# Twelve blocks on one core: the table that orders all steps, written anew

## What is computed

```python
x = x + _L0_xattn_ref(_layernorm(x, axis=-1), ctx_768, ...)
x = x + _L0_attn_ref(_layernorm(x, axis=-1), ...)
x = x + _L0_ffn_ref(_layernorm(x, axis=-1), ...)
...
x = x + _L3_ffn_ref(_layernorm(x, axis=-1), ...)
return x
```

## Time and profile before

| | |
|---|---|
| median of 3 runs | 2554.51 us (2552.6 to 2557.82) |
| span of the profiled execution, first to last instruction | 2557.4 us |
| the profiled execution against the runs | its span is 2.9 us above their median, inside their range |
| instructions | 62,072 |
| constant products in the table | 588 |

### The profile page before, as it was taken

One profiled execution on the slowest core, in us unless ns is written; L12 is line 12 of the kernel. 1 busy time (PEld: TensorE's weight loads), 2 busy tenths in 40 slices (PEclk: granted clock), 3 DMA queues, 4 the chain that ended last, 5 costly groups with the idle time before them and its releaser, 6 DMA issues.

```text
span 2557.4 us, 62072 instructions
## 1 busy us (share of the span) xinstructions
PE 2254.9 (88%) x26420; PEld 1506.9 (59%) x26556; DVE 1746.6 (68%) x4832; ACT 1368.6 (54%) x2287; POOL 774.0 (30%) x676
## 2 busy tenths in 40 slices
...
GB/s 115 19 41 34 80 45 75 42 24 9 9 11 14 8 8 6 1 47 10 17 16 10 19 25 25 25 16 17 10 11 16 58 8 71 40 55 54 55 104 62
DMA packets 50452, 84.14 MB, mean 33 GB/s; under 512 B 9536, under 2 KB 24768, under 8 KB 49792
## 3 DMA queue, kind: packets, MB, share of 16 engines
...
## 4 chain that ended last, share of the span: by engine, by line
PE 57%; DVE 25%; ACT 8%; issue 4%; POOL 3%; DMA 1%; SPq 1%; another core or an unknown queue 0%; DVEq 0%; POOLq 0%; ACTq 0%
PE psum L946 6%; PE psum L908 5%; PE psum L904 5%; PE psum L1606 3%; PE psum L463 2%; DVE c_L3x_most L1726 2%; PE psum L1699 2%; DVE c_L2x_mx L2081 2%; PE psum L1984 2%; DVE c_L2x_p L2087 1%; PE psum L471 1%; PE psum L1395 1%; PE psum L1976 1%; PE psum L773 1%; PE psum L778 1%
## 5 line engine op out<-in xcount | busy, mean ns | idle before, releaser
L893 POOL TENSOR_TENSOR c_L3f_h<-c_L3f_h,c_L3f_spread 128x512 f32<-128x512 f32 x96 | 121.3, 1283 | 188.8 <-DMA c_L3f_spread<-scratch 103.1
L471 PE MATMUL psum<-halves_held 128*128 128x512 bf16 x454 | 131.0, 403 | 14.0 <-issue 9.8
L936 DVE TENSOR_TENSOR c_L3f_h<-c_L3f_h,psum 128x512 f32<-128x512 f32 (+1 forms) x112 | 75.9, 682 | 76.5 <-PE psum L908 52.0
L922 ACT ACTIVATE c_L3f_h<-psum 128x512 f32<-128x512 f32 (+1 forms) x112 | 65.5, 594 | 110.2 <-PE psum L904 99.1
L946 PEld LDWEIGHTS psum<-weights,c_L3f_h 128*128 128x128 f32 (+1 forms) x896 | 108.1, 193 | 19.3 <-issue 15.3
L946 PE MATMUL psum<-weights,c_L3f_h 128*128 128x128 f32 (+1 forms) x896 | 112.9, 279 | 0.0
L904 PE MATMUL psum<-c_L3f_xT,weights 128*128 128x512 f32 x208 | 107.4, 601 | 0.0
L908 PE MATMUL psum<-c_L3f_xT,weights 128*128 128x512 f32 x208 | 107.4, 603 | 0.0
L471 PEld LDWEIGHTS psum<-halves_held 128*128 128x128 bf16 x588 | 54.3, 102 | 74.8 <-issue 35.1
L893 POOL TENSOR_TENSOR c_L0f_h<-c_L0f_h,c_L0f_spread 128x512 f32<-128x512 f32 x64 | 82.5, 1313 | 50.4 <-DVE c_L0f_h L936 39.2
L1606 PE MATMUL psum<-c_L3x_qx,c_L3x_kT 32*128 32x256 f32 x512 | 77.1, 427 | 21.1 <-DVE c_L3x_most L1726 17.4
...
## 6 DMA issues: line engine op xcount, KB each, us to landing
...
```

The costliest lines, as they stand in the source:

```text
L471: nc.tensor.matmul(j.psum[:, bank, :], j.half["ident"], j.half["take"], start=True, stop=True)
L893: nc.gpsimd.tensor_tensor(h, h, j.m["spread"][:, f, :], ALU.mult).then_inc(*j.up("mixed"))
L922: nc.scalar.activation(j.m["h"][P - rows:P, f, :], j.psum[0:rows, 1 + 2 * f % 3, 0:j.tok], ACT.Silu).then_inc(*j.up("silu"))
```

## The change

Only the string `ORDER` is replaced; no function, tile, size or wait is edited, and `PLAN` stays. Two of its 76 lines, one of each:

```diff
 ORDER = (
-    "vqQDDddDVdldkdddp8paglPLaDKQqDpDDLPaApgApGp7PvvdDavAkGKvvpPPP1paVVa3pgdAdaVpgdVlVPp1pA2PGvQvA4PDadvAkPGPlPvdvkV1pVa3pDDA"
...
+    "dddldVkLqdddDDDDqKQDDvDQLldDppaagkPpaPAgApGppvv3PaAGvvVvpPaPPgpaV3pAdagKVVdVPpA1ppvdPAlvaDdl9PAG2PGvkPvvPDDVpQLVadAa3paa"
...
```

138 lines of the change are left out of this document (69 added, 69 removed).

## The result

The changed kernel takes 2564.64 us (median of 20 runs, 2555.8 to 2577.18), the kernel before 2556.8 us on the same chip (20 runs, 2549.33 to 2563.17). The ratio is 1.0032 with a 95% interval of 1.0019 to 1.0044: **slower by 0.32%, some 8 us**, where 18 us of gain were predicted. Each ratio in this text is an estimate of its own from the single fast executions and can differ from the quotient of the two medians by up to 0.14%; one execution of 3741 us of the kernel before (beside experiments 3 and 4) and one of 4532 us (experiment 7) are left out of the ratios as slow.

What follows compares the result with a forecast made beforehand. TensorE's queue was taken as the bound (busy 2254.9 of 2557.4 us); -2 - 3 - 3 - 6 - 4 = -18 us gave 2539.4, less 2.9 for the median: 2536.5 us, forecast 2525 to 2549, whole range 2508 to 2570.

Steps and rivals of the forecast that it cites:

- place A: Kernel start: removing eight constant products ahead of the first transposes moves all that follows by 2.4 us; taken as -2 us.
- the step that began at 796 us: Sign that the forecast is right: this step is reached some 10 us sooner, with a clock above 0.96 from 332 us.
- Idle time, 302.5 us: Whole span: TensorE idle for 302.5 of 2557.4 us, one of two places where an order of steps can win.
- Products elsewhere, -3: Constant products beyond the start, 0.215 us each: half of those added and removed counts, 4.5 us lost, 7.7 gained.
- The clock, -3 at 17%: Second stretch, 332 to 796 us: half clock cost 6.3 us at 17%; half of it comes back with 42 added products.
- Waits of L1a, -6: TensorE's waits in L1a for `topT` (3.4 us) and the maximum (9.0 us): half of the 12.4 us goes.
- Place B: In L1a, L1246 and sixteen L1254 now stand between L1659 and the first L1606, surely removing its 0.69 us wait for `topT`.
- Transfers and moved issues, nothing: SyncE's queue: transfers moved past each other cost nothing, as each is needed by a job a hundred steps or more later.
- The rest, -4 with ends of +25 and -40: Remaining 290 us of TensorE idleness: as many round trips lose cover as gain it, more lost in L2f; little gain, -4 us.
- The rival by the clock in L2f: Fourth stretch, 1138 to 2058 us: 57 fewer constant products bring more half clock, ending slower at 2571 us; chance 0.15.

Runs made afterwards that it cites:

- experiments 3 and 4: Kernel before with, between 1500 and 2120 us, only the new order (1.0044) or counts (1.0042); or new steps 6860 to 7719 (0.9970), also with new start (0.9977).
- experiment 7: Kernel before without its eight starting constant products (1.0029) or with seven (0.9990); changed kernel with the eight put back (1.0037) or old steps 4870 to 6859 (0.9997).
- the new counts in the late part alone: Kernel before, old order everywhere, with the new counts of constant products between 1500 and 2120 us only: 2566.59 us, ratio 1.0042.
- the old late part alone: Changed kernel with the order and counts of before from step 4870 to 6859 (1500 to 2120 us): 2556.83 us, ratio 0.9997.

## Why the prediction was wrong

**The sign.** "Slower" had 0.15, and 2564.64 lies within the range of 2508 to 2570. What bounds the kernel was read rightly: pieces of the order move it by 10 us either way, as TensorE's waits come and go. What failed is the sum: -18 us, beside +8 measured. Of its marks one came, the transposes of place A at 25.81 us for 27.77; the step that began at 796 us came some 5 us later and not 10 sooner.

- **Idle time, 302.5 us.** At most 29 of it, by the gaps some 21, were products without a record. The counts of PE and PEld stood in the earlier trace rows side by side (26420 and 26556), and I didn't read them.
- **Place A, -2.** "The products' going moves all that follows by 2.4 us" failed. It moves the first transposes; the second job's wait for ScalarE's rows, and they came 10.85 us behind the first L552 with the eight products and without, at half clock and at full. The net was nothing by 33 us, and half clock later on made it a loss. The change did win 4.7 us by 233 us, by its other moves (that second L424 starts at 27.46 for 30.85, without a wait for VectorE's L417), but lost it again at 440.
- **Products elsewhere, -3.** The step "I take half of both: 4.5 lost, 7.7 gained" took a product for a cost unless it filled a wait. In the old order the runs say the opposite: without any +82 us, with the new counts +17, with the new counts in the late part alone +8, though one product less costs nothing. In the new order the new counts gain 12 us (ratio 1.0032 for 1.0080, on different chips). No price per product holds for both.
- **The clock, -3 at 17%.** The price came from a piece whose matmuls are small ones (128 L1699, 2.02 us at either clock). The same kernel profiled twice gives 33%, and 342 executions 31%; wide ones pay in full (L1882, 1.95 to 3.75 us). The clock of 332 to 796 us stayed at 0.96, so nothing came back where I had put it, and "in the third and fourth stretches I take no change" left out the 18 to 20 us of half clock that the late part adds.
- **Waits of L1a, -6.** Place B itself came out as foreseen: at 536.37 us the first L1606 behind the sixteen L1254 no longer waits (0.69 before), and the x12 ahead of it waits 0.44 for 1.05. Over the kernel the waits for the maximum fell from 9.0 us to 3.3, but those for `topT` rose from 3.4 to 4.1: 5.0 us of the 12.4 are gone, so this term was about right. It is swamped within the same stretch by two waits I hadn't priced.
- **Transfers and moved issues, nothing.** This is the term that was put at nothing for a reason that doesn't hold: "each is needed by a job that begins a hundred steps or more further on". I looked at the weights. The small transfer of `c_L1x_ctx` had little slack (issued at 431.89, landed 5.2 us later and used at 439.35, 2.2 us behind that), slid behind two more spreads, and its consumer was pulled ahead on VectorE at once. That is a wait of 5.37 us on an engine in whose queue TensorE's next bank was, and costs 3 to 4 us.
- **The rest, -4 with ends of +25 and -40.** Most of the error is here. "In L2f more lost" was seen and given no price. It was +9 in the late part and +4 in the tail against -10 in L3f beside L3x, and the wait and half clock at L1882 are another 4 to 6.
- **The rival by the clock in L2f** (2571) had the right place, since the old late part alone undoes the change, and half of the cause. Its mark, a clock of 0.95 or under between 1138 and 2058 us, was missed (0.96), but over the same work (steps 4850 to 6830) the clock did fall from 0.96 to 0.94. What it had wrong is where the half clock comes from: it named the products removed, and the new order with the old counts has as much. Lost cover comes first, and by the fit above the half clock behind it is the larger part of the cost.

As for the Trainium skill, "TensorE: Matmul & The Clock Gate", section "Why this matters for your kernels": I set its warning of idle gaps aside on the strength of the earlier trace rows. In the kernel before, 12 of the 13 waits of TensorE over 1.8 us (past the first 45 us) have a fall to half clock beside them, the five longest, 3.0 to 8.2 us, among them, and the removal of the wait at 2224 us removed its fall. So the rule agrees here. Shorter waits do it too, though not always: 2.23 us at 440 us in the changed kernel did, and 1.96 us at the same place in the change with the eight products put back didn't (L908 took 1.02 us behind it). And 10 of the 29 falls before have no wait over 1 us near, as that of the earlier trace rows: it isn't the only way.

What stays open: why the eight products at the start are worth 7 to 9 us in the old order, of which half clock explains some 4, and none in the new; what TensorE waits 2.55 us for at L1882; and why either half of the late edit costs what both do.
